# Experts in a fused graph network: one part of 128 slots to a load of weights instead of two

## The chip, the cores and the metric

The kernel runs on one core of a Trainium2 chip, as one launch. The metric is the device time of a whole execution in microseconds (us). Three executions of the kernel before took 3391.48, 3399.17 and 3400.55 us; the median is 3399.17.

## The reference, cut to what matters

The whole computation is a chain of four blocks on 1250 tokens of 768 values: a graph attention network of three layers, a mixture of experts, a graph convolution network, and an attention block with a feed-forward. The change is in the mixture of experts alone. Each token picks its two best of 8 experts, and the result is the sum of their outputs, weighted:

```python
E, C, F, K = (8, 768, 384, 2)
logits = flat @ router_w.T
probs = softmax(logits, axis=-1)
top_w, top_i = top_k(probs, K)
top_w = top_w / top_w.sum(-1, keepdims=True)
for e in range(E):
    w_e = sum(top_w * (top_i == e), axis=-1)[:, None]
    h = gelu(flat @ w1[e] + b1[e])
    out = out + w_e * (h @ w2[e] + b2[e])
```

The reference computes every expert for every token; the kernel computes each chosen pair of token and expert once, 2500 pairs.

## The kernel before, in words

The kernel is a row of stages (`Phase`), each with its own semaphores and closed by a barrier of all engines. Within a stage each engine has its instructions written out in order, and waits on semaphores. The queue of SP issues the plain DMAs, POOL the gathers and scatters. Products are in three passes (`product`, L103): both operands are split into a high part (float32r) and the remainder, and high x high, high x low and low x high are added, so each operand has to be split before use.

`route` (L1003 on) finds for each token its two experts and gives each pair a slot. The slots of an expert begin at a multiple of PER_LOAD x PART = 256, so that a load of weights serves two parts of 128 slots. L999 gives the number of loads that suffice for any choice, LOADS = 17, and PARTS = 34; these are constants of the program. How many loads an expert spans is found by comparing its count with each multiple of 256 (L1164, L1165). Slots that stay empty point to spare rows. `load_expert` holds the expert of each load, `slot_token` and `slot_gate` the token and the weight of each slot, one column a part.

`experts` (L1209 on) then runs over all parts, filled or not:

- SP (`load`, L1255): the first-layer weights w1 (L1259), the bias b1 broadcast to 128 partitions (L1262), the second-layer weights w2 (L1265). There is one staging buffer for w1 and one for w2 (`stock`), so w1 of load n waits until w1 of load n-1 has been split, and w2 likewise.
- ScalarE and VectorE split the weights into two sets of buffers (`w1_pair`, `w2_pair`, chosen by load % 2): ScalarE copies the high part (L1375, L1382), VectorE subtracts it (L1433, L1438), in 6 pieces for w1 and 3 for w2.
- POOL gathers the 128 rows of part n+3 (L1287), and scatters the result of part n into `sum_scratch` with an addition (L1300); each scatter waits for the one before.
- TensorE, for each part n (L1359): `up(n)`, the first layer (L1322, 18 matmuls); `down(n - 1)`, the second layer of the part before (L1343, 18 matmuls); `turn_hidden(n)` (L1331); `turn(n + 2)`, the gathered rows turned (L1311). `up` waits piece by piece for the split of w1.
- ScalarE, for each part n (L1416): Gelu (L1396), `leave(n - 1)`, which scales the result by the gate (L1409), the high part of the turned hidden values (L1402), that of the turned rows of part n+2 (L1389), and then one layer of the next load: the first layer in the first part of a load, the second layer in the second.
- VectorE, for each part n (L1468): bias (L1453), the remainders of hidden values (L1457) and of rows (L1443), and then the same layer of the next load.

So the order of the work is written out by hand on each engine. Before the first part stands load 0, whose rows and layers are split ahead of the loop. At the end SP loads the weights of a later stage ahead (L1275), once the last layer is split.

Of the kernel before, what the change touches and what calls it, by code (L numbers as in the profile page):

```python
# [994 lines left out]

EXPERTS, FF = 8, 384
PART = 128
PER_LOAD = 2
LOADS = (2 * N + EXPERTS * (PER_LOAD * PART - 1)) // (PER_LOAD * PART)  # L999
PARTS = LOADS * PER_LOAD  # L1000


def route(nc, g, i):  # L1003
# [50 lines left out]
    with ph.block() as block:  # L1054
# [67 lines left out]
        def _(v):  # L1122
# [40 lines left out]
            step(v.tensor_scalar(span[:, 0], start[:, NT, :], 0.0, None, ALU.is_gt))  # L1163
            for k in range(1, (N - 1) // (PER_LOAD * PART) + 1):  # L1164
                step(v.scalar_tensor_tensor(span[:, 0], start[:, NT, :], float(k * PER_LOAD * PART), span[:, 0], ALU.is_gt, ALU.add))  # L1165
            step(v.tensor_tensor(lower_span[:], lower[:], span[:, 0].unsqueeze(1).broadcast_to([TP, EXPERTS, EXPERTS]), ALU.mult))
            step(v.tensor_reduce(span[:, 1], lower_span[:], AX.X, ALU.add))
            step(v.tensor_tensor(span[:, 2], span[:, 0], span[:, 1], ALU.add))
            step(v.tensor_scalar(span[:, 3], span[:, 1], float(PER_LOAD * PART), None, ALU.mult))
            v.wait_ge(slots_const, 1)  # L1170
# [38 lines left out]
def experts(nc, g, i, x, token_scratch, sum_scratch, ahead):  # L1209
# [32 lines left out]
    def turned(bank, size):  # L1242

        return ps[:, bank, 0:size].rearrange("p (k n) -> p k n", n=PART)

    with ph.block() as block:

        @block.sync
        def _(sp):
            sp.wait_ge(cleared, 2)  # L1250
            sp.dma_start(b2[0:EXPERTS, :], i["moe_b2"]).then_inc(b2_in, 16)
            sp.dma_start(token_scratch[N:N + PART, :], zeros[:]).then_inc(spare_stored, 16)
            sp.dma_start(sum_scratch[N:N + PART, :], zeros[:]).then_inc(spare_stored, 16)

            def load(n):  # L1255
                e = sp.value_load(load_expert[0:1, n:n + 1], min_val=0, max_val=EXPERTS - 1)
                if n >= 1:
                    sp.wait_ge(w1_split, KD * n)
                sp.dma_start(w1, i["moe_w1"][bass.ds(e, 1)].rearrange("a (k p) f -> p (a k) f", p=128)).then_inc(w1_in, 16)  # L1259
                if n >= 2:  # L1260
                    sp.wait_ge(bias_added, PER_LOAD * (n - 1))
                sp.dma_start(b1[:, n % 2, :], i["moe_b1"][bass.ds(e, 1), :].partition_broadcast(128)).then_inc(b1_in[n % 2], 16)  # L1262
                if n >= 1:
                    sp.wait_ge(w2_split, KF * n)
                sp.dma_start(w2, i["moe_w2"][bass.ds(e, 1)].rearrange("a (k p) f -> p (a k) f", p=128)).then_inc(w2_in, 16)  # L1265

            load(0)
            for t in range(NT):
                sp.wait_ge(b2_added, 2 * t + 2)
                move_rows(sp, sum_scratch[t * TP:(t + 1) * TP, :], x[:, t, :], x_stored)  # L1270
            for n in range(1, LOADS):
                load(n)
            sp.wait_ge(w1_split, KD * LOADS)
            sp.wait_ge(w2_split, KF * LOADS)
            load_ahead(sp, g, ahead, ahead_in)  # L1275
            sp.wait_ge(ahead_in, 16 * len(ahead))
# [91 lines left out]
        @block.scalar  # L1368
        def _(a):
            def first_layer(n):  # L1370
                a.wait_ge(w1_in, 16 * (n + 1))
                if n >= 2:
                    a.wait_ge(up_done, PER_LOAD * (n - 1))
                for k in range(KD):
                    a.activation(w1_pair[:, n % 2, 0, k], w1[:, k], ACT.Copy).then_inc(w1_high, 1)  # L1375

            def second_layer(n):
                a.wait_ge(w2_in, 16 * (n + 1))
                if n >= 2:
                    a.wait_ge(down_done, 2 * PER_LOAD * (n - 1))  # L1380
                for k in range(KF):
                    a.activation(w2_pair[:, n % 2, 0, k], w2[:, k], ACT.Copy).then_inc(w2_high, 1)  # L1382

            def row_tops(n):
                a.wait_ge(row_turned, n + 1)
                if n >= 2:
                    a.wait_ge(up_done, n - 1)
                for ks, bank, size in sides:
                    last = a.activation(rows_T[:, n % 2, 0, ks], turned(bank, size), ACT.Copy)  # L1389
                last.then_inc(row_high, 1)  # L1390

            def gelu(n):
                a.wait_ge(bias_added, n + 1)
                if n >= 2:
                    a.wait_ge(h_turned, n - 1)
                a.activation(hidden[:, n % 2, :], biased[:, n % 2, :], ACT.Gelu).then_inc(gelu_done, 1)  # L1396

            def hidden_tops(n):
                a.wait_ge(h_turned, n + 1)
                if n >= 2:  # L1400
                    a.wait_ge(down_done, 2 * (n - 1))
                a.activation(hidden_T[:, n % 2, 0], turned(TURN, FF), ACT.Copy).then_inc(h_high, 1)  # L1402

            def leave(n):
                if n >= 3:
                    a.wait_ge(y_added, 16 * (n - 2))
                for j in range(2):
                    a.wait_ge(down_done, 2 * n + j + 1)
                    a.activation(y[:, n % 3, j * 384:(j + 1) * 384], ps[:, DOWN + j, 0:384], ACT.Copy,  # L1409
                                 scale=slot_gate[:, n:n + 1]).then_inc(y_ready, 1)  # L1410

            first_layer(0)
            row_tops(0)
            row_tops(1)
            second_layer(0)
            for n in range(PARTS):  # L1416
                gelu(n)
                if n >= 1:
                    leave(n - 1)
                hidden_tops(n)  # L1420
                if n + 2 < PARTS:
                    row_tops(n + 2)
                after = n // PER_LOAD + 1
                if after < LOADS:
                    (first_layer if n % PER_LOAD == 0 else second_layer)(after)
            leave(PARTS - 1)

        @block.vector
        def _(v):
            def first_layer(n):  # L1430
                for k in range(KD):
                    v.wait_ge(w1_high, KD * n + k + 1)
                    v.tensor_tensor(w1_pair[:, n % 2, 1, k], w1[:, k], w1_pair[:, n % 2, 0, k].bitcast(F32), ALU.subtract).then_inc(w1_split, 1)  # L1433

            def second_layer(n):
                for k in range(KF):
                    v.wait_ge(w2_high, KF * n + k + 1)
                    v.tensor_tensor(w2_pair[:, n % 2, 1, k], w2[:, k], w2_pair[:, n % 2, 0, k].bitcast(F32), ALU.subtract).then_inc(w2_split, 1)  # L1438

            def row_rest(n):  # L1440
                v.wait_ge(row_high, n + 1)
                for ks, bank, size in sides:
                    last = v.tensor_tensor(rows_T[:, n % 2, 1, ks], turned(bank, size), rows_T[:, n % 2, 0, ks].bitcast(F32), ALU.subtract)  # L1443
                last.then_inc(row_split, 1)

            def add_bias(n):
                load = n // PER_LOAD
                if n % PER_LOAD == 0:
                    v.wait_ge(b1_in[load % 2], 16 * (load // 2 + 1))
                v.wait_ge(up_done, n + 1)  # L1450
                if n >= 2:
                    v.wait_ge(gelu_done, n - 1)
                v.tensor_tensor(biased[:, n % 2, :], ps[:, UP + n % 2, 0:FF], b1[:, load % 2, :], ALU.add).then_inc(bias_added, 1)  # L1453

            def hidden_rest(n):
                v.wait_ge(h_high, n + 1)
                v.tensor_tensor(hidden_T[:, n % 2, 1], turned(TURN, FF), hidden_T[:, n % 2, 0].bitcast(F32), ALU.subtract).then_inc(h_split, 1)  # L1457

            for t in range(NT):
                for j in range(2):  # L1460
                    v.wait_ge(b2_done, 2 * t + j + 1)
                    here = x[:, t, j * 384:(j + 1) * 384]
                    v.tensor_tensor(here, ps[0:TP, 6 + j, 0:384], here, ALU.add).then_inc(b2_added, 1)
            first_layer(0)
            row_rest(0)
            row_rest(1)
            second_layer(0)
            for n in range(PARTS):  # L1468
                add_bias(n)
                hidden_rest(n)  # L1470
                if n + 2 < PARTS:
                    row_rest(n + 2)
                after = n // PER_LOAD + 1
                if after < LOADS:
                    (first_layer if n % PER_LOAD == 0 else second_layer)(after)
    ph.end()


# [1054 lines left out]
```

## Time and profile before

| what | value |
|---|---|
| median of 3 executions | 3399.17 us |
| the profiled execution, its own time | 3393.07 us |
| its span from first to last instruction | 3391.3 us |
| TensorE busy in the span (matmul) | 2654.1 us, 78% |
| VectorE, ScalarE, POOL busy | 2014.4, 1358.2, 354.3 us |
| mean granted TensorE clock | 0.885 of full speed |
| DMA in the span | 268.25 MB, mean 79 GB/s |

One execution is profiled. Times in it are microseconds from the first instruction; PE is TensorE, PEld its weight loads, which run beside it, DVE VectorE, ACT ScalarE, SPq an instruction of SP's queue. The granted clock is the part of TensorE's full clock (2.4 GHz) that it was given. The ends of matmuls are modelled.

### The profile page before, as it was taken

How to read it: one execution, taken by the hardware profiler on the slowest of the kernel's cores; microseconds unless marked ns; L12 is line 12 of the kernel's file. 1: busy time of each engine (PE TensorE's matmuls, PEld its weight loads, DVE VectorE, ACT ScalarE, POOL GpSimd, SP SyncE). 2: the span in 40 equal slices, each digit the busy share in tenths (PEclk: the TensorE clock that was granted, in tenths of full speed). 3: DMA queues.
4: the chain of work that ended last, by engine and by line, in shares of the span. 5: the costliest groups of instructions: out<-in, count | busy, mean ns of one | idle time of the engine just before them, and what ended most of it. 6: DMA issues, size and time to landing. Idle time of an engine off the chain costs nothing. (4 is left out here: it accounts for less than half of the span.)

```text
span 3391.3 us, 40509 instructions
## 1 busy us (share of the span) xinstructions
PE 2654.1 (78%) x14722; PEld 2336.5 (69%) x14723; DVE 2014.4 (59%) x2944; ACT 1358.2 (40%) x2206; POOL 354.3 (10%) x309
## 2 busy tenths in 40 slices
PE   6666596976976978994899559779796897999777
PEld 5555486876876867883798527467565675888776
DVE  7665457967967963225656415442795454888754
ACT  1223255655756642101566300031695102666420
POOL 1233021012003000000233102000000000111100
PEclk9988797988988988996999769979897896999978
DMA  0010311110111116211899730123561212334214
GB/s 31 15 30 16 87 38 36 54 61 36 54 61 36 53 37 147 55 28 46 277 258 260 187 78 1 46 89 125 132 133 26 92 45 46 80 85 96 56 37 96
DMA packets 107207, 268.25 MB, mean 79 GB/s; under 512 B 10894, under 2 KB 49280, under 8 KB 105806
## 3 DMA queue, kind: packets, MB, share of 16 engines
q1 hardware_dynamic: 99440, 239.43, 26.0%
q0 software_dynamic: 7616, 26.74, 3.6%
q8 instruction: 102, 1.67, 0.2%
q14 instruction: 49, 0.40, 0.0%
HBM read 195.58 MB, written 66.73 MB: 77 GB/s over the span
## 5 line engine op out<-in xcount | busy, mean ns | idle before, releaser
L840 PE MATMUL ps<-h,e_gat_aggregate 125*125 125x193 f32 x2400 | 408.6, 334 | 89.5 <-DVE e_gat_aggregate L824 73.4
L840 PEld LDWEIGHTS ps<-h,e_gat_aggregate 125*125 125x125 f32 x2400 | 402.0, 192 | 96.2 <-DVE e_gat_aggregate L824 77.1
L786 ACT ACTIVATE e_gat_aggregate<-row_gat_aggregate,from_src 125x1250 f32<-125x1250 f32 x120 | 160.7, 1339 | 166.6 <-PE ps L840 139.1
L103 PE MATMUL ps<-gat_w_pair_gat_scores,x_turned 128*125 128x384 f32 x1080 | 196.6, 344 | 39.1 <-DVE gat_w_pair_gat_scores L698 38.7
L822 DVE TENSOR_TENSOR e_gat_aggregate<-e_gat_aggregate 125x1250 f32<-125x1250 f32 x120 | 175.2, 1460 | 86.9 <-DMA gat_bias_gat_aggregate<-in_gat_b 47.8
L103 PEld LDWEIGHTS ps<-gat_w_pair_gat_scores,x_turned 128*125 128x125 f32 x1080 | 194.3, 190 | 41.1 <-DVE gat_w_pair_gat_scores L698 39.9
L314 PE MATMUL ps<-dst_hot_build_adjacency,src_hot_build_adjacency 125*125 125x128 bf16 x2380 | 186.7, 235 | 44.0 <-DVE dst_hot_build_adjacency L267 43.3
L314 PEld LDWEIGHTS ps<-dst_hot_build_adjacency,src_hot_build_adjacency 125*125 125x125 bf16 x2380 | 170.4, 148 | 70.1 <-DVE dst_hot_build_adjacency L267 56.7
L2233 DVE TENSOR_TENSOR p_low_attend<-p_attend,p_high_attend 125x1254 fp32r<-125x1254 f32 x120 | 184.2, 1537 | 45.6 <-ACT p_high_attend L2219 42.8
L103 PE MATMUL ps<-w_pair_dense_rows_from,col_dense_rows_from 128*125 128x384 f32 x1080 | 208.4, 352 | 1.8 <-DVE col_dense_rows_from L962 1.8
L266 DVE TENSOR_SCALAR src_hot_build_adjacency<-ode_iota_build_adjacency,_columns_build_adjacency 125x1250 bf16<-125x1250 f16 x238 | 134.9, 567 | 111.6 <-PE ps L314 75.5
L103 PEld LDWEIGHTS ps<-w_pair_dense_rows_from,col_dense_rows_from 128*125 128x125 f32 x1080 | 197.6, 195 | 2.5 <-DVE col_dense_rows_from L962 2.5
L2212 ACT ACTIVATE p_attend<-ps 125x1254 f32<-125x1254 f32 (+2 forms) x168 | 148.7, 915 | 119.8 <-PE ps L2175 92.6
L1759 DVE TENSOR_SCALAR_CACHE_REDUCE res_attention_statistics<-ps 125x1250 f32<-125x1250 f32 x120 | 174.0, 1459 | 27.2 <-PE ps L1745 21.4
L824 DVE SCALAR_TENSOR_TENSOR e_gat_aggregate<-e_gat_aggregate,count 125x1250 f32<-125x1250 f32 x120 | 175.3, 1461 | 4.2
L103 PE MATMUL ps<-V_home,ln_turned 128*125 128x512 f32 x720 | 170.0, 399 | 7.6 <-DVE V_home L2013 7.6
L1777 ACT ACTIVATE p_attention_statistics<-res_attention_statistics,eak_attention_statistics 125x1250 f32<-125x1250 f32 x120 | 161.1, 1342 | 25.4 <-DVE res_attention_statistics L1759 14.5
L1744 PE MATMUL ps<-V_home 128*125 128x512 f32 x360 | 139.8, 388 | 34.4 <-DMA V_home<-q_scratch 21.6
L103 PEld LDWEIGHTS ps<-V_home,ln_turned 128*125 128x125 f32 x720 | 135.3, 188 | 42.0 <-DVE V_home L2013 7.8
L707 DVE SCALAR_TENSOR_TENSOR peak_gat_scores<-ps,from_src,peak_gat_scores 125x1250 f32<-125x1250 f32 x108 | 156.6, 1512 | 12.4 <-ACTq L671 12.3
L789 ACT ACTIVATE e_gat_aggregate<-row_gat_aggregate,from_src 125x1250 f32<-125x1250 f32 x120 | 158.7, 1323 | 0.9 <-DMA row_gat_aggregate<-r_scratch 0.9
L454 PE MATMUL ps<-ident,_normed_layernorm_turned 125*128 125x125 f32 x300 | 67.2, 400 | 117.3 <-DVE _normed_layernorm_turned L439 117.2
(367 smaller groups left out, 5061.3 us busy)
## 6 DMA issues: line engine op xcount, KB each, us to landing
stock<-in_moe_w SPq DMA_DIRECT2D x34, 1152.0 KB
row_gat_aggregate<-r_scratch SPq DMA_DIRECT2D x24, 625.0 KB, 6.5
V_home<-q_scratch SPq DMA_DIRECT2D x48, 312.5 KB, 6.5
rows_dense_rows_from<-node_scratch SPq DMA_DIRECT2D x10, 1080.0 KB
stock<-in_gat_w SPq DMA_DIRECT2D x4, 2304.0 KB, 8.5
q_scratch<-V_home SPq DMA_DIRECT2D x6, 1250.0 KB, 4.6
k_scratch<-V_home SPq DMA_DIRECT2D x6, 1250.0 KB, 4.5
V_home<-k_scratch SPq DMA_DIRECT2D x24, 312.5 KB, 6.5
```

Of the source, the lines that this page charges most:

```text
L103: last = pe.matmul(out, left(x), right(y), start=start and n == 0, stop=stop and n == 2)
L314: last = pe.matmul(ps[0:TP, 3 * odd + t // 4, t % 4 * 128:t % 4 * 128 + 128], src_hot[:, j, t * TP:(t + 1) * TP], dst_hot[:, j].rearrange( ...
L707: last = v.scalar_tensor_tensor(peak[:, head, :], far[t % 2], from_src[:, head, t:t + 1], peak[:, head, :], ALU.subtract, ALU.min)
L786: a.activation(e[:, n % 3, 0, :], row[0:TP, head % 2, 0, :], ACT.Exp, bias=from_src[:, head, t:t + 1])
L789: a.activation(e[:, n % 3, 1, :], row[0:TP, head % 2, 1, :], ACT.Exp, bias=from_src02[:, head, t:t + 1]).then_inc(exp_ready, 1)
L822: v.tensor_tensor(e[:, n % 3, 0, :], e[:, n % 3, 0, :], e[:, n % 3, 1, :], ALU.max).then_inc(p_step, 1)
L824: v.scalar_tensor_tensor(e[:, n % 3, 0, :], e[:, n % 3, 0, :], 1.0, count[:, t, 0:N], ALU.min, ALU.mult).then_inc(p_ready, 1)
L840: last = pe.matmul(ps[0:TP, bank(head, d // 2), d % 2 * (C + 1):(d % 2 + 1) * (C + 1)], e[:, n % 3, 0, d * TP:(d + 1) * TP], h[:, t, head, :],
L1759: v.tensor_scalar(minus[:, n % 3, :], flat(n), 1.0, None, ALU.mult, ALU.min, accum_out=peak[:, head, t:t + 1]).then_inc(peaked, 1)
L1777: a.activation(p[:], minus[:, n % 3, :], ACT.Exp, scale=-1.0, bias=peak[:, head, t:t + 1], accum_out=total[:, head, t:t + 1]).then_inc(sum ...
L2212: last = a.activation(spread(p[:, n % 2, :])[:, at:end, :], ps[0:TP, bank:bank + end - at, 0:PIECE], ACT.Exp, scale=-1.0)
L2233: v.tensor_tensor(p_low[:, n % 2, :], p[:, n % 2, :], p_high[:, n % 2, :].bitcast(F32), ALU.subtract).then_inc(split, 1)
```

## The change

PER_LOAD goes from 2 to 1. By L999 LOADS becomes (2500 + 8 x 127) / 128 = 27 rounded down, and PARTS 27. An expert's slots begin at a multiple of 128, and every part has a load of its own. In the loops of ScalarE and VectorE both layers of load n+1 now stand at the end of part n. What else uses PER_LOAD follows: `route` compares the counts with the 9 multiples of 128 under 1250 instead of 4 of 256, the waits of ScalarE and SP for buffers count parts instead of pairs, and in `up` and `down` every part waits for its weights. The order of work on TensorE, SP and POOL is as before.

```diff
-PER_LOAD = 2
+PER_LOAD = 1
 LOADS = (2 * N + EXPERTS * (PER_LOAD * PART - 1)) // (PER_LOAD * PART)
 PARTS = LOADS * PER_LOAD
...
                 hidden_tops(n)
                 if n + 2 < PARTS:
                     row_tops(n + 2)
-                after = n // PER_LOAD + 1
-                if after < LOADS:
-                    (first_layer if n % PER_LOAD == 0 else second_layer)(after)
+                if n + 1 < LOADS:
+                    first_layer(n + 1)
+                    second_layer(n + 1)
             leave(PARTS - 1)
...
                 hidden_rest(n)
                 if n + 2 < PARTS:
                     row_rest(n + 2)
-                after = n // PER_LOAD + 1
-                if after < LOADS:
-                    (first_layer if n % PER_LOAD == 0 else second_layer)(after)
+                if n + 1 < LOADS:
+                    first_layer(n + 1)
+                    second_layer(n + 1)
```

## Rows read from the trace of the kernel before

**Rows 1.** The parts of the stage as one stretch: busy us of each engine.

```profile
core 0: us, PE busy (x) PEld busy (x) DVE busy (x) ACT busy (x) POOL busy (x), PEclk, DMA share, GB/s
1641.00:1911.00 270.00, 248.41 (x1500) 241.70 (x1500) 154.58 (x277) 169.16 (x344) 81.95 (x63) 0.99 0.89 247
```

**Rows 2.** Groups by line: busy us, mean ns | idle before, and its releaser.

```profile
L103 PE MATMUL ps<-w_pair_experts,rows_turned_experts 128*128 128x384 f32 x612 | 116.7, 343 | 0.0
L103 PE MATMUL ps<-w_pair_experts,hidden_turned_experts 128*128 128x384 f32 x612 | 111.8, 334 | 1.3 <-DVE hidden_turned_experts L1457 1.3
```

**Rows 3.** Waits of 1700 to 1880 us: total us, times, longest.

```profile
PE ps L1311 <- DMA rows_experts<-token_scratch,slot_token: 13.0, 15, 1.7
```

**Rows 4.** The tile of hidden values: ns min/median/max, first and last start.

```profile
L1396 ACT ACTIVATE hidden_experts<-biased_experts x34: 522/525/528, 1641.8 to 1903.6; 128x384 f32<-128x384 f32 x34
```

**Rows 5.** Order of time, two parts: start us, us, instruction [idle before].

```profile
1753.91 3.39 PE L103 MATMUL ps<-w_pair_experts,rows_turned_experts 128*128 128x384 f32 x18
...
1754.95 2.59 ACT L1375 ACTIVATE w_pair_experts<-stock 128x384 fp32r<-128x384 f32 x6
...
1756.04 2.90 DVE L1433 TENSOR_TENSOR w_pair_experts<-stock,w_pair_experts 128x384 fp32r<-128x384 f32 x6
...
1757.14 3.28 PE L103 MATMUL ps<-w_pair_experts,hidden_turned_experts 128*128 128x384 f32 x18
...
1759.11 0.38 SPq L1259 DMA_DIRECT2D stock<-in_moe_w  x1
...
1759.86 1.18 ACT L1409 ACTIVATE y_experts<-ps,slot_gate 128x384 f32<-128x384 f32 x2
...
1760.26 0.49 PE L1331 MATMUL ps<-ident,hidden_experts 128*128 128x128 f32 x3
1760.94 0.48 ACT L1402 ACTIVATE hidden_turned_experts<-ps 128x384 fp32r<-128x384 f32 x1
...
1761.51 0.88 PE L1311 MATMUL ps<-ident,rows_experts 128*128 128x128 f32 x6 [0.76 <-DMA rows_experts<-token_scratch,slot_token]
...
1762.43 0.87 ACT L1389 ACTIVATE rows_turned_experts<-ps 128x512 fp32r<-128x512 f32 x2 [1.00 <-PE ps L1311]
1763.18 2.31 ACT L1382 ACTIVATE w_pair_experts<-stock 128x768 fp32r<-128x768 f32 x3
...
1764.27 2.69 DVE L1438 TENSOR_TENSOR w_pair_experts<-stock,w_pair_experts 128x768 fp32r<-128x768 f32 x3
...
1766.87 0.55 DVE L1453 TENSOR_TENSOR biased_experts<-ps,b_experts 128x384 f32<-128x384 f32 x1
...
1767.46 0.53 ACT L1396 ACTIVATE hidden_experts<-biased_experts 128x384 f32<-128x384 f32 x1 [1.96 <-DVE biased_experts L1453]
```

**Rows 6.** DMA queues: 1700:1880 (two lines), 1632:1640, 1911:1922; packets, MB, share.

```profile
q1 hardware_dynamic: 15074, 28.79, 49.3%
q0 software_dynamic: 5003, 17.53, 44.5%
...
q1 hardware_dynamic: 1503, 3.14, 100.7%
...
q0 software_dynamic: 288, 0.79, 48.9%
```

**Rows 7.** Order of time, the first load of the stage.

```profile
1614.16 0.41 SPq L1259 DMA_DIRECT2D stock<-in_moe_w  x1
...
1619.90 2.59 ACT L1375 ACTIVATE w_pair_experts<-stock 128x384 fp32r<-128x384 f32 x6 [40.87 <-DMA stock<-in_moe_w]
```

**Rows 8.** Order of time after idle stretches of TensorE, and one microsecond of the second.

```profile
1770.72 0.87 PE L1311 MATMUL ps<-ident,rows_experts 128*128 128x128 f32 x6 [1.74 <-DMA rows_experts<-token_scratch,slot_token]
...
1883.55 1.39 PE L1311 MATMUL ps<-ident,rows_experts 128*128 128x128 f32 x6 [2.29 <-DMA rows_experts<-token_scratch,slot_token]
1884.59 4.54 PE L103 MATMUL ps<-w_pair_experts,rows_turned_experts 128*128 128x384 f32 x18
...
1884.00:1885.00 1.00, 1.00 (x6) 1.00 (x5) 0.00 (x0) 0.03 (x1) 0.77 (x1) 0.50 0.54 215
```

**Rows 9.** The comparisons in route: ns min/median/max, first and last start.

```profile
L1165 DVE SCALAR_TENSOR_TENSOR span_route<-start_route,span_route x4: 166/166/168, 1580.7 to 1581.3; 125x8 f32<-125x8 f32 x4
```

## The prediction

> **What bounds the kernel now.** I began with the stretches of the expert stage, to see which engine is full. Over 1641 to 1911 us TensorE is busy 248 of 270 us at a granted clock of 0.99, ScalarE 169, VectorE 155, and the DMA engines are busy 0.89 of the time at a mean of 247 GB/s [rows 1]. So TensorE bounds the stage, but a second resource, the 16 DMA engines, is almost full behind it. The busy groups by line say what TensorE does: the first-layer products with the rows and the second-layer products with the hidden values, 612 matmuls each, 18 per part of 128 slots [rows 2]. The waits then tell what else delays it: between 1700 and 1880 us it waits 13.0 us in 15 of some 23 parts for gathered rows [rows 3]. The first and the last Gelu of the stage, 1641.8 and 1903.6 us, give the pace: 33 intervals in 261.8 us, 7.93 us each [rows 4].
>
> One part in order of time [rows 5]: TensorE needs 3.39 us for the first layer, 3.28 for the second layer of the part before, 0.49 to turn hidden values, 0.88 to turn the rows of the part after the next, 8.04 in all. That sum is what recurs every 7.93 us (the 0.1 more is the modelled ends of matmuls). In one part ScalarE and VectorE split the first layer of the next load, in the next part its second layer, so each pair of parts pays for one load of weights.
>
> **What the change removes.** 34 parts become 27. Seven parts of 8.04 us are 56 us less of TensorE work, seven gathers and seven scatters go too. If TensorE stayed the bound, this would be the gain.
>
> **What it adds.** 17 loads become 27, and each part must now take a whole load. Per part, ScalarE does 2.59 (first layer) + 2.31 (second) + 0.53 (Gelu) + 1.18 (results) + 0.48 (hidden tops) + 0.87 (row tops) = 7.96 us, VectorE 2.90 + 2.69 + 0.55 = 6.1 us and the remainders of rows and hidden values besides [rows 5]. Three engines at 8 us each or less would still fit into 8 us if nothing depended on anything. But the weights are split only one part ahead, and in the new order first and second layer of load n+1 both stand before the bias of part n+1 on VectorE.
>
> **The chain of engines per part.** I set zero where ScalarE begins the first layer of the next load, 1754.95 in the row. VectorE begins 1.09 later and needs 0.48 a piece (2.90 for six), so the first piece is split at about 1.65. There first layer products of the next part start, paced by 3 matmuls a piece: 1.65 + 3.39 = 5.04. The second layer of the part now finished takes to 8.3, the turn of hidden values to 8.8, the turn of rows to 9.7, and ScalarE's row tops (0.87) to 10.6, when it may start the next first layer. VectorE's own path is shorter: 1.09 + 2.90 + 2.69 + 0.55 = 7.2 to the bias, 7.8 with the Gelu, so Gelu is ready before the turn that wants it. The period of this chain is thus 10.6 us, not 8: the 1.65 before the first split piece and the 0.87 of the row tops are covered now (the products of the part run on weights split one part or two earlier) and are not covered afterwards. It leaves out any wait for a transfer. The row waits of 13.0 us [rows 3] vanish, since a gather issued one part ahead gets 10 us instead of 8.
>
> **The DMA engines per part.** A load is 2 x 1152 KB and 192 KB of biases broadcast, 2.556 MB; gather and scatter come on top. Alone on the engines weights ran at 3.14 MB in 8 us, 392 GB/s [rows 6], so a load is 6.5 us at the least. In the stage, mixed with rows, the weight queue took 49.3% of 180 us for 28.79 MB, which is 7.88 us for a load, and the row queue 44.5% of 180 us for some 23 parts, 3.48 us a part [rows 6]. A scatter alone at the end cost 0.489 x 11 / 2 = 2.7 us (two of them in 0.79 MB) [rows 6], so the 3.48 is hardly a product of contention. Before, two parts needed 7.88 + 6.96 = 14.8 of 15.9 us. After, one part needs between 6.5 + 3.5 = 10.0 (clean) and 7.88 + 3.48 = 11.4 us (loaded), whatever the engines do. At the 0.94 that the loaded shares reach now (49.3 + 44.5) it is 12.1.
>
> Does a transfer fit into the chain? The one staging buffer for each layer is free when VectorE has split its last piece (first layer 4.0, second 6.7 after zero), and SP issues 0.17 later [rows 5]. The first layer has until 10.6, that is 6.4 us; the very first one took from 1614.16 to 1619.90, 5.7 us [rows 7]. The second layer has from 6.9 to 13.2, but its bytes queue behind those of the first and the biases, and the part's scatter, issued once the results are written at about 9.1, wants the same engines. By the clean price that just fits; by the loaded price it doesn't, and ScalarE then waits in front of one of the two layers. I take 11.7 us a part, the middle of 11.4 and 12.1, since the traffic will be at least as mixed as in the stage now, and keep 10.6 (chain) and 12.1 for the range.
>
> The Trainium skill, "DMA: Bandwidth & Descriptors" (section Bandwidth), puts the ceiling of the fabric at 435 GB/s. By that figure the 3.34 MB of a part would be 7.7 us, an estimate, and the DMA engines would never bind, which would make rival 1 below the result; the trace disagrees, with 392 GB/s for weights and about 150 for a scatter.
>
> **TensorE's clock.** TensorE will be idle from 9.7 to 12.25 in each period, 2.5 us. Idle for 1.74 us left the next turn of rows at 0.87 us; idle for 2.29 us made it 1.39 and the next first layer 4.54 in place of 3.39, with a granted clock of 0.50, which is 1.2 GHz [rows 8]. That is 1.66 us, and TensorE is on the new chain. I count it at nothing in the forecast, since slack towards the DMA bound (11.7 less 10.6) hides most of it, and as a rival beyond.
>
> **Small terms.** Route gets 5 more comparisons at 0.166 us [rows 9], +0.8 us; its tables of 27 instead of 34 columns are priced at nothing, as are the first load (same instructions) and the load ahead for the next stage (issued at the last part but one, with some 20 us left). The issues on SP rise by 30, of under 0.4 us each, on a queue that only waits. POOL's scatter waits for the one before it, at most 8.4 us to land, under the new period.
>
> **Sum.** 27 parts have 26 intervals, each with a load: 26 x 11.7 = 304.2, less 261.8, plus 0.8, is +43 us. Against the profiled execution's 3393.1 us that is 3436; the median of the runs shown, 3399.2, lies 6 higher than that one execution, and I split the difference: 3439 us. The bounds: 26 x 10.6 = 275.6 gives +15, 26 x 12.1 gives +54.
>
> **Rivals.**
> 1. The engine chain alone, transfers hidden at the clean price: 10.6 us a part, +15 us, 3408 to 3414. For it: clean sum 10.0 is under 10.6. Against: it leaves the engines 0.6 us free in each part, in a stage where they show 0.94 already. Chance 0.20.
> 2. The clock falls in each part on top of late transfers: 11.7 + 1.66 = 13.4 us, +87 us, 3480 to 3486. For it: the idle gap of 2.5 us or more comes in every part. Against: of the gaps now only the longest did it, and a slow stretch hidden in the wait for weights costs nothing. Chance 0.25, with longer ones in it. The Trainium skill, "TensorE: Matmul & The Clock Gate" (section HAM oscillation), says the same of loops that wait for a DMA: every tile can start cold. By that rule this rival is the likeliest; the trace has one fall of this kind, so I don't make it the forecast.
> 3. The other side, faster: TensorE stays the bound at 7.93 us, 26 x 7.93 = 206, -56 us, 3337 to 3343. Its place is the hiding of split and transfer behind TensorE. It decides when the period falls under 261.8 / 26 = 10.1 us, that is, if transfers of a part take less than 10.1 and the split overlaps more than I have drawn. Against: 3.34 MB in 7.93 us would be 421 GB/s, over anything here, and the chain sum of 10.6 has each step in a row. Chance of ending over 10 us faster: 0.04.
> That the counts don't come out as said is excluded: both are constants of the formula, (2500 + 1016) / 128 = 27.
>
> **How the numbers follow.** Forecast 0.46; rival 1 0.20; rival 2 0.25; within 0.3% (10 us, about what this kernel's runs can tell from no change) 0.05, a period of 9.7 to 10.4; faster 0.04. The range from 3406 to 3484 takes in both bounds and rival 2. Faster 0.04, same 0.05, slower 0.91.
>
> **What would show it.** Gelu to Gelu 11 to 12 us; TensorE idle before the first-layer products for some 3 us a part; ScalarE with a wait for the staged weights, absent now between parts; DMA share near 0.95 or more with more than 280 GB/s; the waits for gathered rows gone. If ScalarE never waits for the weights, the forecast's reason is wrong even if the time is right. If first layers take 4.5 us part after part at a clock of 0.5, rival 2 holds. A period under 10 would refute the chain.

## The result, and the profile after

The changed kernel took 3436.54 to 3447.45 us in 4 runs, median 3440.47, beside 3398.32 for the kernel before in runs on the same chip (4 runs, 3391.48 to 3400.55). The ratio is 1.0129, with a 95% interval of 1.0112 to 1.0146: slower by about 42 us. The profiled execution took 3436.54 us, with a span of 3434.8. Nearly all of the loss lies in the expert stage: the stage starts within a microsecond of where it did, the stage behind it begins 40.5 us later (its first load at 1963.91 in place of 1923.37), and what follows that load takes 3.0 us longer in this pair of executions.

The stage as a whole, the same stretch as in [rows 1] and then 1700 to 1880 us:

```profile
core 0: us, PE busy (x) PEld busy (x) DVE busy (x) ACT busy (x) POOL busy (x), PEclk, DMA share, GB/s
1641.00:1911.00 270.00, 200.45 (x1036) 192.24 (x1035) 173.21 (x298) 174.90 (x343) 56.69 (x44) 0.89 0.93 280
...
1700.00:1880.00 180.00, 131.43 (x684) 125.49 (x684) 115.09 (x199) 117.69 (x234) 40.21 (x31) 0.89 0.95 287
```

TensorE fell from 248 busy microseconds of 270 to 200, and its granted clock from 0.99 to 0.89. The DMA engines went from 247 to 280 GB/s. The fullest resource has changed.

The Gelu of the stage, which gives the pace as [rows 4] did, with the maximum and minimum of its duration and its first and last start:

```profile
L1396 ACT ACTIVATE hidden_experts<-biased_experts x27: 522/525/527, 1642.2 to 1945.0; 128x384 f32<-128x384 f32 x27
```

26 intervals in 302.8 us are 11.65 us a part; before it was 7.93 with 33 intervals in 261.8. The difference of the two stretches, 41.0 us, is nearly the whole of the loss.

Who waited for whom between 1700 and 1880 us (total us, times, longest), some 15.5 parts:

```profile
PE ps L103 <- DVE w_pair_experts L1433: 41.3, 15, 4.1
...
ACT w_pair_experts L1382 <- DMA stock<-in_moe_w: 23.8, 14, 3.2
DVE w_pair_experts L1438 <- ACT w_pair_experts L1382: 20.1, 12, 3.2
...
ACT w_pair_experts L1375 <- DMA stock<-in_moe_w: 4.8, 6, 1.9
```

The wait for gathered rows of [rows 3] is gone, in its place TensorE waits 2.75 us a part for the first piece of the split, and ScalarE waits 1.85 us a part for a staged layer, mostly for the second. The DMA queues in the same stretch, as in [rows 6]:

```profile
q1 hardware_dynamic: 20642, 39.79, 66.6%
q0 software_dynamic: 3360, 11.80, 27.7%
```

A load of 2.556 MB takes 0.666 x 180 x 2.556 / 39.79 = 7.70 us of all 16 engines, the rows of a part (0.762 MB, the 17.53 MB before over some 23 parts) 0.277 x 180 x 0.762 / 11.80 = 3.22 us, 10.9 in all, of a period of 11.65. The 128 rows of 768 values of a part, gathered and scattered, are 0.786 MB exactly, which would make it 3.32 us; I keep 0.762 so that the prices here compare with those of the prediction.

One part in order of time (start, length, instruction, idle before it and its releaser):

```profile
1774.34 2.58 ACT L1375 ACTIVATE w_pair_experts<-stock 128x384 fp32r<-128x384 f32 x6
...
1776.14 4.95 PE L103 MATMUL ps<-w_pair_experts,rows_turned_experts 128*128 128x384 f32 x18 [2.59 <-DVE w_pair_experts L1433]
...
1780.92 3.31 PE L103 MATMUL ps<-w_pair_experts,hidden_turned_experts 128*128 128x384 f32 x18
...
1785.25 0.87 ACT L1389 ACTIVATE rows_turned_experts<-ps 128x512 fp32r<-128x512 f32 x2
...
1786.20 2.59 ACT L1375 ACTIVATE w_pair_experts<-stock 128x384 fp32r<-128x384 f32 x6
...
1790.69 2.32 ACT L1382 ACTIVATE w_pair_experts<-stock 128x768 fp32r<-128x768 f32 x3 [1.90 <-DMA stock<-in_moe_w]
```

In the part from 1774.34 to 1786.20 us no transfer is late, yet it takes 11.86 us: the first layer runs at 4.95 us instead of 3.39, after 2.59 us of idle TensorE. So the trace offers two causes that fit the same 11.65: the transfers (10.9 us, ScalarE waits for them), and the engine chain with a slowed first layer (11.4 to 11.9). Of 25 first layers listed from 1655 to 1945 us, 18 took 4.67 to 5.89 us and 7 took 3.36 or 3.38. The experiments were made to tell the two apart.

### The profile page after: what moved, and what is told of

Read it like the earlier page. It is cut to its first block and busy times, and to the rows that moved or that the text cites. A ratio compares the mean times of both kernels' runs of the same rounds, so it can differ in the third digit from the quotient of the medians.

```text
span 3434.8 us, 40042 instructions
## 1 busy us (share of the span) xinstructions
PE 2633.5 (77%) x14407; PEld 2314.6 (67%) x14408; DVE 2059.3 (60%) x3011; ACT 1388.5 (40%) x2254; POOL 337.9 (10%) x295
## 5 line engine op out<-in xcount | busy, mean ns | idle before, releaser
L786 ACT ACTIVATE e_gat_aggregate<-row_gat_aggregate,from_src 125x1250 f32<-125x1250 f32 x120 | 160.6, 1339 | 166.3 <-PE ps L840 139.9
L103 PE MATMUL ps<-w_pair_experts,rows_turned_experts 128*128 128x384 f32 x486 | 122.6, 422 | 69.9 <-DVE w_pair_experts L1433 69.9
L103 PEld LDWEIGHTS ps<-w_pair_experts,rows_turned_experts 128*128 128x128 f32 x486 | 114.6, 252 | 75.2 <-DVE rows_turned_experts L1443 64.7
```

Of the source, the lines that this page charges most:

```text
L103: last = pe.matmul(out, left(x), right(y), start=start and n == 0, stop=stop and n == 2)
L786: a.activation(e[:, n % 3, 0, :], row[0:TP, head % 2, 0, :], ACT.Exp, bias=from_src[:, head, t:t + 1])
```

## The experiments

Each kernel ran beside the kernel before on the same chip; ratios are to it. Periods are from the first and last Gelu, by 26 intervals (33 where there are 34 parts).

### The slow clock alone

```diff
                 if n + 2 < PARTS:
                     turn(n + 2)
+                for _ in range(16):
+                    pe.transpose(ps[:, 7, 0:PART], ident[:], ident[:])
```

> The changed kernel with 16 transposes of the identity into an unused bank of PSUM behind each part's turn of rows, some 2.3 us of work in TensorE's gap of 2.6 us, so that its clock stays up. Theory D (the transfers set the period of 11.65 us, the slow clock costs nothing): 3440 us as the changed kernel, within 4 us, and ScalarE waits longer for the staged weights. Theory C (the engine chain with a first layer slowed from 3.39 to 4.95 us sets it): the period falls towards the chain's 10.6 us, to 3413 to 3425 us, first layers take 3.4 us again and TensorE's granted clock in the stage is 0.98 or more.

Measured: 3439.3 us (3434.4 to 3442.4), ratio 1.0117 (1.0094 to 1.0140). The windows row of 1700 to 1880 us, and the group of first-layer matmuls in it (busy us, mean ns, idle before):

```profile
1700.00:1880.00 180.00, 146.18 (x915) 140.39 (x915) 116.57 (x199) 115.82 (x228) 38.67 (x30) 0.96 0.93 281
...
L103 PE MATMUL ps<-w_pair_experts,rows_turned_experts 128*128 128x384 f32 x270 | 52.3, 347 | 16.8 <-DVE w_pair_experts L1435 16.8
```

The matmuls are back at 347 ns from 419 (the mean in the changed kernel from 1655 to 1930 us) and the clock is at 0.96, and the time is that of the changed kernel. What the clock gave back went into waits: ScalarE waits 24.9 + 9.2 us for the weights where it waited 28.6, and TensorE 17.0 us for Gelu where it waited 5.9. Theory C falls; the slow clock is real and costs nothing here, where something else holds the period.

The list of first layers in the changed kernel says the same. From one first layer to the next a part with a slow one takes 11.84 us in the mean, and a part with a fast one 11.5 (the last part left out), although the fast one is some 1.4 us shorter. In the next run, where the transfers are thin, the same difference is kept: 11.4 and 10.05 us.

### Thin transfers, without and with the clock

```diff
+                k1, k2 = (KD, KF) if n < 2 else (1, 1)
-                sp.dma_start(w1, i["moe_w1"][bass.ds(e, 1)]...
+                sp.dma_start(w1[:, 0:k1, :], i["moe_w1"][bass.ds(e, 1), 0:k1 * 128, :]...
-                sp.dma_start(w2, i["moe_w2"][bass.ds(e, 1)]...
+                sp.dma_start(w2[:, 0:k2, :], i["moe_w2"][bass.ds(e, 1), 0:k2 * 128, :]...
```

> The changed kernel, but from the third load on only 1/6 of w1 and 1/3 of w2 is transferred (the stale rest is split and multiplied as before), so that a load is 0.79 MB in place of 2.56 MB. Theory D: the period falls to the engine chain of 10.6 us, 26 x 1.05 = 27 us less, about 3413 us. Theory C: ScalarE's wait for weights goes, yet the clock still falls in each part and the period stays at 11.4 to 12.0 us, 3434 to 3449 us.

> Both of the two before: thin loads and TensorE kept busy in the gap. Both theories: the bare engine chain, 10.6 us a part, 3413 us; over 11.2 us a part the chain was drawn too short, under 10.2 too long.

Measured: 3400.7 us, ratio 1.0009 (0.9998 to 1.0020); with TensorE kept busy as well 3395.9 us, ratio 0.9989 (0.9975 to 1.0003). The periods, 10.26 and 10.00 us:

```profile
L1397 ACT ACTIVATE hidden_experts<-biased_experts x27: 522/525/528, 1647.8 to 1914.6; 128x384 f32<-128x384 f32 x27
```

```profile
L1399 ACT ACTIVATE hidden_experts<-biased_experts x27: 522/526/527, 1643.1 to 1903.1; 128x384 f32<-128x384 f32 x27
```

Taking the bytes away gives back 40 of the 42 us, 12 more than theory D expected: the transfers are what the changed kernel pays for. It also shows what is left. The bare engine chain is 10.0 us a part, not the 10.6 that I had drawn, and with it the changed kernel is as fast as the one before and no faster. Where most of the 0.6 went can be read in the run with thin transfers:

```profile
1755.14 2.58 ACT L1376 ACTIVATE w_pair_experts<-stock 128x384 fp32r<-128x384 f32 x6
...
1756.92 3.38 PE L103 MATMUL ps<-w_pair_experts,rows_turned_experts 128*128 128x384 f32 x18 [2.58 <-DVE w_pair_experts L1434]
...
1760.14 3.28 PE L103 MATMUL ps<-w_pair_experts,hidden_turned_experts 128*128 128x384 f32 x18
...
1763.26 0.49 PE L1332 MATMUL ps<-ident,hidden_experts 128*128 128x128 f32 x3
...
1763.59 0.82 PE L1312 MATMUL ps<-ident,rows_experts 128*128 128x128 f32 x6
...
1764.44 0.87 ACT L1390 ACTIVATE rows_turned_experts<-ps 128x512 fp32r<-128x512 f32 x2
1765.20 2.58 ACT L1376 ACTIVATE w_pair_experts<-stock 128x384 fp32r<-128x384 f32 x6
```

From start to start the steps are 3.22, 3.12, 0.33 and 0.85 us, where the lengths are 3.38, 3.28, 0.49 and 0.82: the next group starts while the modelled end of the last still runs. Three links on TensorE were each some 0.16 us too long in my sum, and the row tops (0.87) overlap the next copy by 0.11. Against that, the first split piece comes 1.78 us after the copy begins, where I had 1.65. The part takes 10.06 us.

### The transfers alone

```diff
+                pieces = KD if n < 2 else 1
-                for k in range(KD):
-                    a.activation(w1_pair[:, n % 2, 0, k], w1[:, k], ACT.Copy).then_inc(w1_high, 1)
+                for k in range(pieces):
+                    a.activation(w1_pair[:, n % 2, 0, k], w1[:, k], ACT.Copy).then_inc(w1_high, KD // pieces)
```

and the same for the second layer and on VectorE.

> The changed kernel with whole transfers, but from the third load on only the first of the 6 and the first of the 3 pieces is split, so the staging buffers come free early and ScalarE and VectorE have 4 us less a part. What is left is TensorE's 8.04 us or the transfers, whichever is longer. Theory D (loaded price of the prediction): a period of 11.4 us or more, 3434 us or more. Theory C (clean price): 10.0 to 10.6 us, 3397 to 3413 us. A period of 8 to 9 us (3345 to 3371) would mean that the transfers are not near any limit.

Measured: 3421.8 us, ratio 1.0072 (1.0046 to 1.0098), a period of (1929.0 - 1645.1) / 26 = 10.92 us. The stretch and the queues of 1700 to 1880 us:

```profile
1700.00:1880.00 180.00, 134.48 (x737) 130.07 (x736) 57.20 (x97) 68.38 (x131) 41.25 (x32) 0.92 1.00 303
...
q1 hardware_dynamic: 21854, 41.82, 66.6%
q0 software_dynamic: 3597, 12.62, 32.7%
```

ScalarE and VectorE are idle most of the time and the DMA engines are at 1.00. By the shares a load is 0.666 x 180 x 2.556 / 41.82 = 7.33 us and the rows of a part 0.327 x 180 x 0.762 / 12.62 = 3.55, 10.9 together, which is the period, as it must be where the shares fill it. It lies between the two theories, 10.6 and 11.4: for this mix of traffic the clean price was 0.9 too low, the loaded one 0.5 too high.

### A second staging buffer, without and with the clock

```diff
-                if n >= 1:
-                    sp.wait_ge(w1_split, KD * n)
-                sp.dma_start(w1, i["moe_w1"]...
+                if n >= 2:
+                    sp.wait_ge(w1_split, KD * (n - 1))
+                sp.dma_start(w1s[n % 2], i["moe_w1"]...
```

and so for w2; the splits read `w1s[n % 2]` and `w2s[n % 2]`, and each buffer has a semaphore of its own.

> The changed kernel with a second staging buffer for each layer, so that the transfers of a load run one part further ahead and no longer wait for the split of the load just before. Theory H (the 11.65 us a part are the 10.92 that the transfers need by themselves, plus time in which the DMA engines stand idle because a staging buffer is not yet free): period 10.9 to 11.0 us, 26 x 0.7 = 18 us less, about 3421 us. Theory M (the extra is the mixing of weight and row traffic and of the clock): no change, 3436 to 3444 us.

> Two staging buffers for each layer, and TensorE kept busy in its gap. If the 10.78 us a part of the run with two buffers are the transfers alone (10.6 us by their shares), nothing changes: 3411 to 3421 us. If the slow clock is part of them, up to 26 x 0.7 less: 3398 to 3408 us.

Measured: 3416.9 us (3413.6 to 3422.5), ratio 1.0061 (1.0041 to 1.0081), period 10.78 us. With TensorE kept busy 3404.2 us (3397.0 to 3415.4), ratio 1.0014 (0.9999 to 1.0029), period 10.45. The stretch of 1700 to 1880 us, with two buffers and then with two buffers and the clock:

```profile
1700.00:1880.00 180.00, 133.46 (x741) 128.41 (x742) 125.76 (x219) 126.10 (x251) 43.56 (x34) 0.94 0.98 307
```

```profile
1700.00:1880.00 180.00, 158.07 (x1032) 151.34 (x1031) 125.69 (x221) 126.86 (x255) 43.83 (x34) 1.00 1.01 316
```

The DMA share goes from 0.95 to 0.98 and 1.01, and in these 180 us ScalarE waits for the weights in neither run. The buffers are worth 24 us (3440.5 less 3416.9), and the time is 4 us under the 3421 that theory H expected. Only a part of that is the idle time of which theory H speaks. By the shares, the time in which the DMA engines stood idle fell from 0.05 x 11.65 = 0.58 us a part to 0.02 x 10.78 = 0.22, and the time in which they were busy for the same bytes from 11.07 to 10.56. The second is more than half of the gain, and no run gives its cause; the mixing of traffic that theory M names is not excluded for it.

And now the clock does matter, by 13 us more (16 by the ratios, since the two runs were on different chips), which the prediction had at nothing; the second branch of the expectation holds. What sets the two periods can be read from the traces. With two buffers 10 of 26 first layers are slow by some 1.4 us, 0.5 us a part, and TensorE waits 2.9 us in 17 parts for gathered rows: 10.0 + 0.5 + 0.2 = 10.7 of 10.78. With the clock held none is slow, and the wait for rows between 1700 and 1880 us is

```profile
PE ps L1312 <- DMA rows_experts<-token_scratch,slot_token: 7.6, 8, 1.8
```

which is 0.45 us a part, and 10.0 + 0.45 is the period of 10.45. So the full transfers still cost something, but through the rows and no longer through the weights; and since every byte was moved in 10.45 us a part, the 10.9 of the section before is no lower limit. Both kernels compute the full result, and the better one comes to the time of the kernel before, not under it.

### Scatters that write, without and with the clock

```diff
-                                        in_=y[:, n % 3, :], in_offset=None, compute_op=ALU.add).then_inc(y_added, 16)
+                                        in_=y[:, n % 3, :], in_offset=None).then_inc(y_added, 16)
```

> The changed kernel with the scatter writing its rows instead of adding them (the sum over a token's two experts is left out). Theory D (the transfers bind): if the addition is what makes a scatter cost 2.7 us of the DMA engines and a plain one costs about 1.0, a part needs 9.2 us of transfers and the period falls to near the engine chain of 10.0, 10.1 to 10.5 us, 3400 to 3411 us. If it is the indirect rows that cost, or if the transfers do not bind, 3436 to 3444 us.

> Scatters that write instead of adding, and TensorE kept busy in its gap. Theory K (with the transfers eased it is the engine chain, lengthened by the slow clock to some 11.4 us, that holds the period at 11.39): the period falls to 10.1 to 10.5, 3396 to 3407 us. Theory S (the single staging buffers hold it, since a layer's transfer begins only after its split and ends 3 us late in some parts): 3418 to 3428 us.

Measured: 3424.4 us, ratio 1.0075 (1.0055 to 1.0094), period 11.39; with the clock 3428.0 us, ratio 1.0073 (1.0046 to 1.0100), period 11.43. The stretch and queues of the first:

```profile
1700.00:1880.00 180.00, 131.57 (x697) 126.29 (x698) 118.84 (x207) 119.38 (x236) 30.81 (x32) 0.89 0.86 288
...
q1 hardware_dynamic: 20234, 39.19, 66.1%
q0 software_dynamic: 2560, 12.58, 19.7%
```

The row queue takes 0.197 x 11.39 = 2.24 us a part instead of 0.277 x 11.65 = 3.23, so the addition itself costs about 1.0 us of the engines, less than the 1.7 I had put down. But only 16 us came back instead of 29 to 40, and the DMA share fell to 0.86. By the traces 7 of them lie between the first and the last Gelu (302.8 to 296.1 us) and 4.5 behind the last (18.9 to 14.4 us until the next stage begins), where the stage waits for its last scatters. Theory K (the clock) is refuted by the second run, whose clock is at 0.97. Theory S is what remains, and the trace shows its cycle, here for the second layer (SPq issues its transfer, ScalarE copies it, SPq issues the next):

```profile
1765.57 0.37 SPq L1265 DMA_DIRECT2D stock<-in_moe_w  x1
...
1775.29 2.31 ACT L1382 ACTIVATE w_pair_experts<-stock 128x768 fp32r<-128x768 f32 x3 [3.50 <-DMA stock<-in_moe_w]
1776.17 2.69 DVE L1438 TENSOR_TENSOR w_pair_experts<-stock,w_pair_experts 128x768 fp32r<-128x768 f32 x3 [3.19 <-ACT w_pair_experts L1382]
...
1778.89 0.37 SPq L1265 DMA_DIRECT2D stock<-in_moe_w  x1
```

9.7 us from issue to use, behind the first layer's 1.4 MB and beside the rows, then 3.6 us of splitting in which the buffer is closed: 13.3 us for that round, against a mean period of 11.39.

### All three

> All three: two staging buffers, scatters that write, TensorE kept busy. Both theories: transfers of 9.5 us under an engine chain of 10.0 us, so the period is the chain's, 10.0 to 10.2 us, 3393 to 3401 us: no faster than the kernel before. A period over 10.5 would mean that a limit is missing from the account.

Two buffers, scatters that write and TensorE kept busy: 3397.5 us, ratio 0.9989 (0.9978 to 1.0001), period (1903.4 - 1642.2) / 26 = 10.05 us. This is the bare engine chain again, reached with every byte of the weights transferred, though without the sums over a token's two experts. Beside the run with scatters that write and the clock alone (3428.0 us, on the same chip) the two buffers are worth 30 us, which is theory S tested by itself. No limit of the period is missing from the account.

### The order of the change without its loads

```diff
                 after = n // PER_LOAD + 1
-                if after < LOADS:
-                    (first_layer if n % PER_LOAD == 0 else second_layer)(after)
+                if after < LOADS and n % PER_LOAD == 0:
+                    first_layer(after)
+                    second_layer(after)
```

on the kernel before, with its 34 parts and 17 loads, on both engines.

> The kernel before (34 parts, 17 loads) with both layers of the next load split in the first part of each pair, and none in the second: the order of the change without its extra loads. Theory chain: the first part of a pair then costs 10.0 us in place of 7.93, 16 x 2.1 = 33 us more, about 3431 us. Rival: the second part of the pair gives the time back, 3395 to 3402 us.

Measured: 3455.8 us (3447.7 to 3462.6), ratio 1.0178 (1.0157 to 1.0200). The sign is that of the theory, the size nearly double: 60 us, (1957.3 - 1636.3) / 33 = 9.73 us a part, 3.6 us more for each pair. One pair shows where it goes beyond the chain:

```profile
1761.04 3.29 PE L103 MATMUL ps<-w_pair_experts,hidden_turned_experts 128*128 128x384 f32 x18
...
1765.37 0.55 DVE L1454 TENSOR_TENSOR biased_experts<-ps,b_experts 128x384 f32<-128x384 f32 x1
...
1766.53 0.55 PE L1331 MATMUL ps<-ident,hidden_experts 128*128 128x128 f32 x3 [2.21 <-ACT hidden_experts L1396]
...
1767.49 4.97 PE L103 MATMUL ps<-w_pair_experts,rows_turned_experts 128*128 128x384 f32 x18
...
1777.15 0.87 PE L1311 MATMUL ps<-ident,rows_experts 128*128 128x128 f32 x6 [1.25 <-DMA rows_experts<-token_scratch,slot_token]
```

The first layer of the next part was done before 1761.2, but its bias stands on VectorE behind 5.6 us of splitting and comes at 1765.4. TensorE waits for Gelu, its clock falls, and the gathered rows are late again. The waits add up to the 3.6 us: between 1700 and 1880 us TensorE waits 18.3 us for Gelu and 18.5 us for rows in some 9 pairs, 4.0 us a pair, where the kernel before waits 1.1 us a pair for rows, and the first layers are 0.8 us a pair slower (364 in place of 343 ns a matmul). The order of the splits alone costs more than the change as a whole, at a DMA share of 0.77.

### Gathers one part earlier, on the kernel before

```diff
-            for n in range(3):
+            for n in range(4):
                 fetch(n)
             for n in range(PARTS):
-                if n + 3 < PARTS:
-                    fetch(n + 3)
+                if n + 4 < PARTS:
+                    fetch(n + 4)
```

> The kernel before with rows gathered four parts ahead instead of three (the four buffers allow it). If the wait of TensorE for gathered rows, 13.0 us in 180, is the lateness of the issue: up to 0.072 x 262 = 19 us less, 3379 to 3385 us. If the DMA engines, 0.94 full, are the reason, the wait moves elsewhere: 3393 to 3400 us.

Measured: 3390.2 us, ratio 0.9982 (0.9970 to 0.9994), the only run under the kernel before by more than its interval, by 6 us. The waits of 1700 to 1880 us:

```profile
POOL sum_scratch L1300 <- DMA sum_scratch<-y_experts,slot_token: 97.9, 19, 7.4
...
PE ps L1311 <- DMA rows_experts<-token_scratch,slot_token: 12.6, 10, 2.2
```

In this stretch TensorE's wait for rows hardly changed, 12.6 us where it was 13.0. Over all parts (1641 to 1900 us) it fell from 18.9 to 12.6 us, which is the size of the gain; the Gelus show 7 us (261.8 to 254.4). POOL now waits 97.9 us for the landing of the scatter before, where it waited 22.0, and only 16.7 for the results of ScalarE, where it waited 89.3. So two thirds of the wait for rows is not the lateness of the issue. That the full DMA engines are its reason fits, and is not shown. The time lies between the two expectations.

## Why the prediction was right

The time (3439 forecast, 3440.5 measured), the direction and the mechanism held: the transfers hold the period, with the engine chain under them. That the time came within 2 us is luck, as the third step shows. By its steps:

- **What the change removes and what it adds.** The decomposition is now measured. At TensorE's old pace, 26 intervals of 7.93 would be 206 us, 56 less than before. The engine chain of 10.0 us (run with thin transfers and clock) makes them 260: this chain, with both layers split in every part, takes back 54 of the 56. The transfers and their buffers make them 303, the remaining 43.
- **The engine chain, 10.6 us.** Too long by 0.6: I added lengths of rows with modelled ends where only start to start counts. The same reading stands behind the 8.04 us of the kernel before: it is not 7.93 and modelled ends alone, but overlaps of 0.16 at the links and, against them, 0.57 us a part of waiting for rows (13.0 us in 22.7 parts). The forecast did not rest on the 10.6, its rival did, and with 10.0 that rival would have been the case of no change.
- **The transfers, 11.4 us loaded, 10.0 clean.** 10.9 measured, with the engines at 1.00, and 10.45 with two buffers and the clock, at 1.01. So the loaded price was 0.5 to 0.9 too high. Why is open: a price taken from the share of a queue is no constant. A load took 7.88 us before, 7.33 in the transfers alone and 7.67 with two buffers and the clock; the rows of a part took 3.48, 3.55 and 2.92, and 4.0 with thin transfers, where the engines had the least to do. I then allowed for the 0.94 at which the engines can be kept, got 12.1, and took the middle, 11.7. With the 10.9 the product would have been 10.9 / 0.94 = 11.6. A share taken too dear and a middle taken too low cancelled.
- **Why only 0.94.** The prediction took the number over from the stage before without a reason. For the changed kernel the single staging buffers are a reason: with two of each the share goes from 0.95 to 0.98, and 24 us come back, less than half of them as idle time of the engines.
- **The clock at nothing.** Right for this kernel, where keeping the clock up changed 1 us, and for the stated reason, that the transfers hold the period. It was not hidden altogether elsewhere: with two buffers it is worth 13 us, with thin transfers 5. Rival 2 named what happened in most parts (4.95 us for a first layer), so that its own sign, first layers of 4.5 us part after part, was met, and priced it wrongly as an addition to the wait for weights. The Trainium skill, on its page "TensorE: Matmul & The Clock Gate" (section HAM oscillation), says that a loop whose matmuls wait for a DMA in every tile starts every tile cold. The 18 slow of 25 here agree with that in the main, though what TensorE waited for was the split piece (2.59 us), and 7 parts were not cold. A cold start counts only where TensorE is on the path.
- **The row waits vanish**, as written. **The small terms:** route has 9 comparisons in place of 4 and is otherwise too small to see in the runs.
- **Faster (0.04).** It did not come, and the runs show why: even with the transfers thinned, the chain of 10.0 us a part lies only just under the 10.1 at which the change would break even.

## What to carry to other kernels

Fewer padded parts are worth only what the new period leaves of them: work out the period of the dependency chain from start to start, then that of the transfers with every byte on the engines, and take the larger, before multiplying by the smaller count. Here the number of parts fell by a fifth, while the period of the engines rose by a quarter (7.93 to 10.0 us), because the split of the first piece and the row tops are no longer covered, and the bytes of weights rose by three fifths. With one staging buffer for each tensor the transfers did not reach their own limit here (shares of 0.95, and 0.86 where the scatters wrote): try a second one before concluding that bandwidth binds. In this kernel a repair of TensorE's clock was worth 1 us before that and 13 us after.

## What the runs showed of the hardware that I had not expected

- Idle stretches of TensorE of the same length did not do the same to its clock: 2.59 us before a first layer of 4.95 us in the changed kernel, 2.58 us before one of 3.38 us in the run with thin transfers, whose clock was 0.98 over 180 us. Even there 6 of 26 first layers were slow, behind the same 2.58 us or less. A difference between the two runs is the period, 11.65 and 10.26 us; whether it matters was not tried.
- A scatter that adds cost the DMA engines some 1.0 us more for 0.39 MB than one that writes, and its landing (the median over the stage) took 6.7 us against 4.8. With two buffers and the clock the difference is the same, 0.283 x 10.45 = 2.96 against 0.188 x 10.05 = 1.89 us.
- Weights and rows together ran at 303 GB/s over 180 us where only the transfers held the period (DMA share 1.00), at 316 GB/s with two buffers and the clock (1.01), both with additions, and at 330 GB/s where the scatters wrote as well (0.98). So a share of 1.00 did not mean one rate.
